# Gates folded by GpSimd into the tables of the first stage, in twelve pieces a head, and a recurrence without those products

## The reference

```python
q = silu(conv(x @ Wq)); k = silu(conv(x @ Wk)) * DK**-0.5; v = silu(conv(x @ Wv))
a = sigmoid(x @ Wa + ba); beta = sigmoid(x @ Wb + bb)
# per batch and head, over the 512 steps, with St a 128 x 128 state
err = St @ k_t - v_t
St = a_t[..., None] * St - (b_t[..., None] * err)[..., None] * k_t[:, :, None, :]
o_t = St @ q_t
# then
x = layernorm(x + ((norm(o) * ln_w + ln_b) * sigmoid(x @ Wg)) @ Wo)
x = layernorm(x + (silu(x @ wu.T) * (x @ wg.T)) @ wd.T)   # ternary wu, wg, wd
```

## Time and profile before

| what | us |
|---|---|
| median of 3 runs (2783.69 to 2802.97) | 2786.15 |
| the profiled execution, device time | 2792.46 |
| its span, first to last instruction | 2790.7 |
| projections, from the span's start | 932.7 |
| recurrence, from 932.7 to 2036.9 | 1104.2 |
| attention_out and feed-forward, the rest | 753.8 |

### The profile page before, as it was taken

One profiled execution on the slowest core, in us unless ns is written; L12 is line 12 of the kernel. 1 busy time (PEld: TensorE's weight loads), 2 busy tenths in 40 slices (PEclk: granted clock), 3 DMA queues, 4 the chain that ended last, 5 costly groups with the idle time before them and its releaser, 6 DMA issues. The chain is left out here.

```text
span 2790.7 us, 50619 instructions
## 1 busy us (share of the span) xinstructions
PE 2578.7 (92%) x17812; PEld 2216.3 (79%) x17922; DVE 2042.4 (73%) x5887; ACT 1204.5 (43%) x2393; POOL 1445.2 (52%) x1216
## 2 busy tenths in 40 slices
...
PEclk9999999999999799999999999989859999999999
...
GB/s 132 129 177 185 150 146 163 187 143 146 171 179 124 266 201 215 200 198 198 215 227 231 214 230 227 214 197 198 240 202 158 213 188 122 67 12 11 11 11 15
DMA packets 417321, 454.39 MB, mean 163 GB/s; under 512 B 122497, under 2 KB 367233, under 8 KB 393857
## 3 DMA queue, kind: packets, MB, share of 16 engines
...
HBM read 321.49 MB, written 131.14 MB: 162 GB/s over the span
## 5 line engine op out<-in xcount | busy, mean ns | idle before, releaser
L355 PE MATMUL pa_ps<-pa_x_hi,pa_w_hi 128*128 128x512 f32 x1296 | 507.0, 391 | 9.4 <-ACT pa_y L298 5.2
L355 PE MATMUL pa_ps<-pa_x_lo,pa_w_hi 128*128 128x512 f32 x1296 | 505.1, 390 | 0.0
L355 PE MATMUL pa_ps<-pa_x_hi,pa_w_lo 128*128 128x512 f32 x1296 | 504.9, 390 | 0.0
L438 DVE SCALAR_TENSOR_TENSOR pa_cv<-pa_y,pa_taps,pa_cv 128x2048 f32<-128x2048 f32 x144 | 357.1, 2480 | 17.8
L1197 DVE TENSOR_TENSOR pb_tmp<-pb_gb,pb_ps 128x112 f32<-128x112 f32 (+6 forms) x1792 | 328.5, 221 | 25.5 <-POOL pb_gb L787 11.6
L787 POOL TENSOR_TENSOR pb_gb<-pb_gb,pb_ng 128x448 f32<-128x448 f32 (+6 forms) x448 | 331.6, 786 | 2.9 <-DMA pb_gb<-scratch_pairs 2.9
L1202 DVE TENSOR_TENSOR pb_ps<-pb_ps,pb_tmp 128x112 f32<-128x112 f32 (+6 forms) x1792 | 330.8, 226 | 0.0
L355 PEld LDWEIGHTS pa_ps<-pa_x_hi,pa_w_hi 128*128 128x128 f32 x1296 | 243.6, 188 | 67.1 <-ACT pa_y L298 9.4
L771 POOL TENSOR_TENSOR all_res<-all_res,pb_crow 128x1024 f32<-128x1024 f32 x120 | 281.9, 2367 | 6.1 <-DMA pb_crow<-scratch_crow 6.1
L355 PEld LDWEIGHTS pa_ps<-pa_x_hi,pa_w_lo 128*128 128x128 f32 x1296 | 243.7, 188 | 50.7
L355 PEld LDWEIGHTS pa_ps<-pa_x_lo,pa_w_hi 128*128 128x128 f32 x1296 | 243.6, 188 | 50.0
(11 more groups left out here) (191 smaller groups left out, 5426.9 us busy)
## 6 DMA issues: line engine op xcount, KB each, us to landing
...
pa_o_ng<-scratch_beta SPq DMA_DIRECT2D x16, 1024.0 KB, 7.9
scratch_ng<-pa_o_ng SPq DMA_DIRECT2D x16, 1024.0 KB, 4.5
scratch_A<-pa_o_A SPq DMA_DIRECT2D x16, 1024.0 KB, 4.5
scratch_vt<-pa_o_vt SPq DMA_DIRECT2D x16, 1024.0 KB, 4.5
scratch_q<-pa_o_q SPq DMA_DIRECT2D x16, 1024.0 KB, 6.9
scratch_g<-pa_o_g SPq DMA_DIRECT2D x16, 1024.0 KB, 7.8
```

Of the source, the lines that this page charges most:

```text
L355: last = nc.tensor.matmul(out, w[:, mat, k, :], xx[:, k, b * S:(b + 1) * S], start=(k == 0 and n == 0), stop=(k == KT - 1 and n == 2))
L438: nc.vector.scalar_tensor_tensor(out=out, in0=yy[:, :, k:k + S], scalar=tap(k), in1=out, op0=ALU.mult, op1=ALU.add).then_inc(s_tap, 1)
```

## The change

In projections POOL makes twelve more multiplications a head, 33 steps for 21: `vt` times `ng` in four pieces of 128x512, `cg` = `ng` times the running block decay in four pieces of 128x512, and `rg` = `ng` (of blocks 2 to 4) times the single block decay in four pieces of 128x384. `cg` lies in the memory of `ra`, `rg` in that of `cv[0]`, the convolution of V. `scaled_v` waits for the first 21 steps. SP stores the two new tables, and loads the next beta after the store of `rg`. ACT's exp waits for the store of `cg`, the taps of V for that of `rg`.

In recurrence `start` multiplies by `cg` (loaded into `W`), `cross` by `rg`, so that w comes with its gate; `solve` begins without the product L1188, and `w_of` is gone. ACT's copy `ngx` goes, the filler matmuls go (except in the last chunk), and SP loads two tables for each half chunk (0.5 and 0.375 MB).

```diff
+        outs["cg"] = ra[:, :, :].rearrange("p b s -> p (b s)").rearrange("p (c b t) -> p c b t", c=NCH, b=B)
+        outs["rg"] = cv[0][:, :, :].rearrange("p b s -> p (b s)")[:, 0:TOK * (CH - BL) // CH].rearrange("p (c b t) -> p c b t", c=NCH, b=B)
-        N_PR = 21
+        N_PR, N_VT, N_CG = 33, 21, 29
...
-                sp.wait_ge(s_pr, N_PR * (h + 1))
+                sp.wait_ge(s_pr, N_PR * h + N_CG)
                 store("A")
+                store("cg")
...
                 if left >= 2:
                     weights(h + 2)
+                sp.wait_ge(s_pr, N_PR * (h + 1))
+                store("rg")
+                if left >= 1:
+                    load_beta(h + 1)
                 sp.wait_ge(s_g, 4 * h + 8)
                 store("g")
...
+                pool.wait_ge(s_ng, h + 1)
+                for c in range(0, NCH, 4):
+                    part = slice(CT * c, CT * (c + 4))
+                    mul(flat(tI)[:, part], flat(tI)[:, part], flat(outs["ng"])[:, part], k if c == 0 else None)
+                assert n[0] == N_VT
                 for j in range(1, NBL):
...
+                pool.wait_ge(s_pr, N_PR * h + k)
+                for c in range(0, NCH * B, 16):
+                    mul(by_block(outs["cg"])[:, c:c + 16], by_block(outs["ng"])[:, c:c + 16], scale(1)[:, c:c + 16])
+                assert n[0] == N_CG
+                pool.wait_ge(s_vt, h + 1)
+                pool.wait_ge(s_st["ng"], 16 * h + 16)
+                for c in range(0, NCH * B, 16):
+                    mul(by_block(outs["rg"])[:, c:c + 16], by_block(outs["ng"])[:, c:c + 16, 1:, :], scale(0)[:, c:c + 16, 1:, :])
...
                     act.wait_ge(s_pr, N_PR * h)
+                    act.wait_ge(s_st["cg"], 16 * h)
...
-                dve.wait_ge(s_pr, N_PR * (h + 1))
+                dve.wait_ge(s_pr, N_PR * h + N_VT)
...
-        FILL = [2, 2, 2, 2, 2, 2, 2, 2]
+        FILL = [0, 0, 0, 0, 0, 0, 0, 0]
...
+            def load_gates(c, hf):
+                half = slice(HALF * hf, HALF * (hf + 1))
+                for name, dst in (("cg", W), ("rg", rg)):
+                    src = flat(scr[name][c, :, :, :]).rearrange("p (h t) -> p h t", h=HB)[:, half, :]
+                    sp.dma_start(flat(dst[:, half, :]), flat(src)).then_inc(s_gl[hf], 16)
...
-                tt(w_of[hf][:, 8 * q:8 * q + 8, :], src[:, :, 0, 0:BL], rr[p][:, 1, hs, 0:1].broadcast_to([P, 8, BL]), ALU.mult)
-                tt(blocks(W[:, hs, :])[:, :, 1:, :], blocks(src[:, :, 0, :])[:, :, 1:, :], cr[:, :, 1:, :], ALU.mult)
+                tt(x_of[hf][:, 8 * q:8 * q + 8, :], src[:, :, 0, 0:BL], W[:, hs, 0:BL], ALU.mult)
+                tt(W[:, hs, BL:], src[:, :, 0, BL:], W[:, hs, BL:], ALU.mult)
...
-                tt(xs, ws, gates, ALU.mult).then_inc(s_sv, 1)
...
-                    rb = groups(rr[p][:, 0, hs, n + 1:n + 2]).broadcast_to([P, 8, 4, BL])
-                    tt(groups(w_of[hf]), src[:, :, 1, :, :], rb, ALU.mult).then_inc(s_wn[hf], 1)
+                    tt(groups(x_of[hf]), src[:, :, 1, :, :], groups(rg[:, hs, BL * n:BL * (n + 1)]), ALU.mult).then_inc(s_wn[hf], 1)
```

More of the change, by code:

```diff
@@ L118, in projections @@
         s_vt = m.sem("vt")
-        s_st = {n: m.sem(f"st_{n}") for n in ("q", "k", "ng", "vt", "A", "g", "r")}
+        s_st = {n: m.sem(f"st_{n}") for n in ("q", "k", "ng", "vt", "A", "g", "r", "rg", "cg")}
         x_rows = x.rearrange("b (s p) d -> (b s) p d", p=P)
@@ L161, in weights, with load_beta, head @@
                     sp.dma_start(w_in[:, mat, :, :], w_dram[mat][:, h, :, :]).then_inc(s_w[mat], 16)
-            def head(h, first, left):
-                if not first:
-                    sp.wait_ge(s_st["ng"], 16 * h)
+            def load_beta(h):
                 sp.dma_start(outs["ng"][:, :, :, :].rearrange("p c b t -> p (c b t)"),
                              scr["beta"][h, :].partition_broadcast(P)).then_inc(s_bb, 16)
+            def head(h, first, left):
                 def store(n):
@@ L255, in head @@
                     k = mul(rv[:, 1, :, :, j:j + 1], before, rv[:, 0, :, :, j:j + 1], k)
[L256 removed]
+                k = step(nc.gpsimd.tensor_copy(rv[:, 1, :, :, 0:1], rv[:, 0, :, :, 0:1]))
+                scale = lambda i: r_out[:, i, :, :, :].rearrange("p c b n -> p (c b) n").unsqueeze(3).broadcast_to([P, NCH * B, NBL, BL])
+                pool.wait_ge(s_pr, N_PR * h + k)
[6 more added lines that the diff above has]
+                    mul(by_block(outs["rg"])[:, c:c + 16], by_block(outs["ng"])[:, c:c + 16, 1:, :], scale(0)[:, c:c + 16, 1:, :])
                 assert n[0] == N_PR
@@ L431, in taps_of @@
                         dve.wait_ge(s_zero, 3)
+                        if not first:
+                            dve.wait_ge(s_st["rg"], 16 * h)
                     yy, out = y[YB[mat]], cv[n][:, :, :]
@@ L513, in recurrence @@
         gb = [m.sb(f"gb{i}", [P, HB, PAIRS]) for i in range(NBL)]
-        ngx = m.sb("ngx", [P, HALF, CH // 2])
+        rg = m.sb("rg", [P, HB, CH - BL])
         tmp = m.sb("tmp", [P, HB, BL - 1])
@@ L519, in recurrence @@
         psT, psD, wx = ps[0:2], ps[2:6], ps[6:8]
-        w_of = [t[:, 0:HALF * BL].rearrange("p (h t) -> p h t", t=BL) for t in wx]
-        x_of = [t[:, HALF * BL:2 * HALF * BL].rearrange("p (h t) -> p h t", t=BL) for t in wx]
+        x_of = [t[:, 0:HALF * BL].rearrange("p (h t) -> p h t", t=BL) for t in wx]
         s_id = m.sem("id")
@@ L546, in recurrence @@
         s_sv = m.sem("sv")
-        s_ngx = m.sem("ngx")
+        s_gl = [m.sem(f"gl{i}") for i in range(2)]
         s_rs = [m.sem(f"rs{i}") for i in range(2)]
@@ L586, in recurrence @@
         turn = lambda c, n, hf: 2 * NBL * c + [[0, 2, 3, 5], [4, 6, 7, 9]][hf][n] - 1
-        scaled = lambda c, n, hf: 27 * turn(c, n, hf) + 1
         @block.sync
@@ L641, in cycle @@
                 if kind != FIRST:
+                    sp.wait_ge(s_wn[1], 6 * c)
+                    load_gates(c, 1)
                     sp.wait_ge(s_x[1], solved(c - 1, 3))
@@ L697, in _ @@
             load_rr(0, 0)
+            for hf in range(2):
+                load_gates(0, hf)
             sp.dma_start(all_decays, scr["r"][1, :, :, :, :, :].rearrange("c p h b n -> p c (h b n)")).then_inc(s_cr, 16)
@@ L923, in cycle @@
                 absolutes(2)
-                act.wait_ge(s_ngl, 16 * (c + 1))
-                if kind != FIRST:
-                    act.wait_ge(s_sv, scaled(c - 1, 3, 1))
-                nc.scalar.activation(ngx[:, :, :], ng[:, HALF:HB, CH // 2:CH], ACT.Copy).then_inc(s_ngx, 1)
                 copy_x(at, past, c, 2, 0)
@@ L1179, in solve @@
                     dve.wait_ge(s_w, 2 * c + hf + 1)
-                    dve.wait_ge(s_ngl, 16 * (c + 1))
                 else:
                     dve.wait_ge(s_wn[hf], 6 * c + 2 * n)
-                gates = ng[:, HALF * hf:HALF * (hf + 1), BL * n:BL * (n + 1)]
-                if hf and n >= NBL // 2:
-                    dve.wait_ge(s_ngx, c + 1)
-                    gates = ngx[:, :, BL * n - CH // 2:BL * (n + 1) - CH // 2]
-                ws, xs = w_of[hf], x_of[hf]
-                tt(xs, ws, gates, ALU.mult).then_inc(s_sv, 1)
+                xs = x_of[hf]
                 dve.wait_ge(s_m, NBL * c + n + 1)
-                dve.wait_ge(s_sv, 27 * k + 1)
                 quarters = [(q, slice(QUART * q, QUART * (q + 1)), slice(QUART * (2 * hf + q), QUART * (2 * hf + q + 1))) for q in range(2)]
@@ L1215, in cross @@
                     dve.wait_ge(s_wv, 2 * c + hf + 1)
-                    tt(w_of[hf], w_of[hf], W[:, hs, BL * (n + 1):BL * (n + 2)], ALU.add).then_inc(s_wn[hf], 1)
+                    tt(x_of[hf], x_of[hf], W[:, hs, BL * (n + 1):BL * (n + 2)], ALU.add).then_inc(s_wn[hf], 1)
             def state(at, c, r):
```

21 lines of the change are left out of this document (13 added, 8 removed).

## The result

The changed kernel takes 2922.74 us (median of 4 runs, 2917.51 to 2928.66) beside 2786.24 us for the kernel before (median of 4): ratio 1.0476, 95% interval 1.0437 to 1.0516. It is slower, by 136.5 us between the medians, where I forecast 98.

The account below looks back on a forecast made before the run. PE paces projections and DVE's row, with short waits for PE, recurrence; DVE and POOL take turns. Terms: 141 + 10 + 5 - 58 = +98 us, 2884 us against the runs' median; range 2795 to 2960.

Parts of the forecast that it names:

- The period: Projections, one head between successive z: set by DVE's row, 64.6 us for 55.2, +141 us over 15 periods.
- the sooner beta: Projections: beta loaded earlier, L452 10 us after z for 13.5; 3.5 us won, 2.5 given back in turns with POOL.
- The single price: Projections: what one POOL piece costs DVE, 1.05 us for 128x512 and 0.75 us for 128x384.
- Two of my signs: Profile after, projections: DVE busy over 50 us a head, and L452 about 10 us after z.
- the rival (c), a ring through POOL: Projections: POOL's lateness carries into the next head, 68 to 70 us a head, about +162, 2948 us; chance 0.08.
- The last head's end: End of projections: waits for the pieces delay recurrence's beginning by +10 us (5 to 15).
- The start of recurrence: Start of recurrence: extra table loads stand ahead of the decay table and Gram stores, +5 us (0 to 8).
- Recurrence: Recurrence phase: DVE loses 128 products L1188, -58 us (ends -70 and -35), before the +5 at its start.
- PE has room: Recurrence: PE can keep up with DVE's shorter row, as filler matmuls go that had 52.2 us recorded.
- (a): Projections: the pieces hide beside DVE, 54.8 us a head; in all -56, 2730 us; chance 0.08.
- (b): Projections: half the turns, pieces fall in DVE's pauses, period grows 3 us; in all -4, 2782 us; chance 0.08.
- (d): Recurrence: without filler the clock falls to 0.87 and the 58 us are lost; +156, 2942 us; chance 0.06.

## Why the prediction was right, and which of its terms were not

I forecast slower by 98 us and 2795 to 2960 us in all; it is slower by 136.5 between the medians (124.7 between the profiled executions), and 2922.74 us lies inside the range. The direction and its cause held: GpSimd's pieces and VectorE's two-input instructions take turns, DVE's row sets the period, and the gain in recurrence is far smaller than the loss. That the period came out to a few tenths is luck, as the first term shows. Term by term:

**The period.** Forecast 64.6 us, measured 64.3: +131.7 us over fifteen for +141. But two terms in it were off, by 6.6 and 6.2 us, and happened to cancel. The pieces were to lengthen DVE's row by 11.4, and by 2.5 more for the sooner beta, less 1 beside z, 12.9 in all; they lengthened it by 6.3. The single price was right where it applies (1.0 us for each piece on `vt`, by the run with these alone), but I let all twelve pay it, and the last eight added 0.3 each on balance. Beta was to come 3.5 us sooner; the waits for it grew instead, 10.7 us a head for 8.9, since SP's queue stands behind the eighth piece, and `vt` added 0.9. So 6.3 + 1.8 + 0.9 = 9.0 us a head, for a period 8.8 longer. Two of my signs failed with it: DVE is busy 48.0 us a head and not over 50, and `ng` begins 11.3 and 20.0 us after z's end in turn and not 10. I had put POOL's last step at 2 us before the issue of beta in every head; it alternates, 1.8 and 10.5 us from z's end to the issue. The rival (c), a ring through POOL, was in part this, at some 2 us a head and not 4 to 5.

**The last head's end.** Forecast +10 (5 to 15), measured +21.2, outside my ends. I had added up DVE's row, but the first load of recurrence hangs on SP's queue. Its last stretch, before and then after:

```profile
912.83 0.37 SPq L170 DMA_DIRECT2D scratch_A<-pa_o_A  x1
...
932.67 0.35 SPq L592 DMA_DIRECT2D pb_kq<-scratch_k  x1
```
```profile
1061.45 0.37 SPq L171 DMA_DIRECT2D scratch_A<-pa_o_A  x1
...
1086.83 0.36 SPq L616 DMA_DIRECT2D pb_kq<-scratch_k  x1
```

The store of A goes out as soon as POOL's counted step is there: 39.1 us after the last z before (the 21st step), 54.7 after (the eighth piece), so +15.6. From there the queue takes 19.8 us before and 25.4 after, with two more tables to store: +5.5, and as much with the new recurrence alone. I noted that beta had come early in that head, and it now comes 9.7 us later (`ng` begins 18.0 us after z for 8.3); but POOL's pieces didn't wait for it, since `ng` was ready at 1029.7 and the first piece began at 1035.0, so that delay isn't on this path.

**The start of recurrence.** Forecast +5 (0 to 8), measured +7.3. The part that I meant was right: from the first load to the first `first_v` 27.4 us pass for 22.0, +5.4, and with the old recurrence behind the new projections it is 22.0 again. The other 1.9 lie in the piece that varies from run to run.

**Recurrence.** Forecast -58 (ends -70 and -35), measured -41.7 in the loop of the profiled executions. About 13 of these belong to the clock, since the kernel before has six chunks below 1.00 there and the kernel after none; between chunks at 1.00 the gain is 64.2 - 62.3 = 1.9 us, -28 over fifteen, outside my near end. The products themselves were priced right: such a chunk has 3.2 us less of DVE's instructions and 0.7 less of the gaps between them, 59 us over fifteen. What I took as nothing is the wait for PE: I had written that PE has room. After, over the loop (beside the earlier trace rows):

```profile
DVE all_res L1244 <- PE pb_ps L1076: 43.4, 31, 2.4
DVE pb_ps L1196 <- PE pb_ps L1038: 34.6, 43, 1.0
DVE pb_ps L1232 <- PE pb_ps L1063: 10.8, 30, 0.4
```

Together 88.8 us for 69.8 (29.5 + 27.9 and 12.4 in a third row). In chunks at a clock of 1.00 the waits grow more, from 3.8 to 5.9 us, which over fifteen gives 31 of the 59 us back. PE is the other half of that to and fro: busy 58.9 of 62.3 us, it has less to spare than DVE had to give.

**The rest.** +5.0 us lie behind the loop, 2.7 of them in `attention_out` and 2.2 behind it, where the code is unchanged; this stretch varied between 810.5 and 815.1 us over the kernels run, and was 809.2 before. What it is stays open.

**Rivals.** (a) and (b) fell: the period is 64.3 us and not 54.8 or some 58, and a piece on `vt` is felt at 1.0 us, which is most of the 1.15 us that it lasts by a quarter of the large product (4.61 / 4, an estimate). (d) fell for this kernel: the clock was 1.00 over the loop, and the filler's return gained nothing. That it can fall without the filler the run with four pieces shows, in two chunks.
